# Two Mamba scans and a binarised convolution block on one core: another order of the kernel's head, and the convolutions' input in two float32r parts in place of three bf16 parts

## What is computed

```python
def _mamba(x, W_in, conv_w, conv_b, W_x, W_dt, b_dt, A_log, D_skip, W_out):
    xc, z = split(x @ W_in.T)                      # 256 features each
    xc = silu(causal_conv4(xc, conv_w) + conv_b)   # along 32 steps
    dbc = xc @ W_x.T                               # 8 for dt, 16 for B, 16 for C
    dt = softplus(dbc[..., :8] @ W_dt.T + b_dt)
    h = exp(dt * A) * h + (dt * xc) * B            # 16 states per feature, step by step
    y = (sum over states of h * C + xc * D_skip) * silu(z)
    return y @ W_out.T

def quantize_w1bit(w): return mean(abs(w)) * sign(w)
out = relu(batch_norm(x, gamma0, beta0))
out = conv3x3(out, quantize_w1bit(w0))
out = relu(batch_norm(out, gamma1, beta1))
out = conv3x3(out, quantize_w1bit(w1)) + x
```

## Time and profile before

| | |
|---|---|
| median of 3 runs | 888.1 us (886.25 to 889.18) |
| the profiled execution | 886.25 us, its span 884.5 us |
| mean granted TensorE clock | 0.959 of full speed |
| busy: PE, PEld, DVE, ACT, POOL | 777.8, 367.0, 764.4, 728.2, 707.7 us |

### The profile page before, as it was taken

One profiled execution on the slowest core, in us unless ns is written; L12 is line 12 of the kernel. 1 busy time (PEld: TensorE's weight loads), 2 busy tenths in 40 slices (PEclk: granted clock), 3 DMA queues, 4 the chain that ended last, 5 costly groups with the idle time before them and its releaser, 6 DMA issues.

```text
span 884.5 us, 13300 instructions
## 1 busy us (share of the span) xinstructions
PE 777.8 (88%) x4606; PEld 367.0 (41%) x4614; DVE 764.4 (86%) x504; ACT 728.2 (82%) x1305; POOL 707.7 (80%) x331
## 2 busy tenths in 40 slices
PE   5776989898999998989999989899999867689898
PEld 3433434343444443434544435354444334244343
DVE  2198999999999999999999999999999999871441
ACT  2798999999999999999999999999999995350310
POOL 0478899999999999999999999999999999300000
PEclk9888999999999999999999999999999987989999
DMA  6606152434242434443434344344444350000011
GB/s 191 253 36 241 49 182 107 177 136 185 106 176 114 167 124 154 159 156 134 151 138 146 144 130 184 126 164 128 161 122 168 113 200 1 1 1 1 0 48 48
DMA packets 39147, 110.99 MB, mean 125 GB/s; under 512 B 7244, under 2 KB 9384, under 8 KB 39080
## 3 DMA queue, kind: packets, MB, share of 16 engines
q1 hardware_dynamic: 36896, 109.81, 34.6%
q10 hardware_dynamic: 2184, 0.33, 0.2%
HBM read 106.97 MB, written 3.15 MB: 125 GB/s over the span
## 4 chain that ended last, share of the span: by engine, by line
DVE 39%; PE 21%; issue 19%; ACT 17%; POOL 2%; ACTq 0%; DMA 0%; POOLq 0%; DVEq 0%
DVE state L763 19%; DVE bank L763 15%; PE bank L1108 11%; ACT product L597 5%; ACT bank L573 4%; ACT state L584 4%; PE bank L959 3%; DVE state L773 2%; PE bank L952 2%; POOL state L511 2%; PE bank L1043 1%; PE bank L894 1%; ACT dt L627 1%; ACT L622 1%; PE bank L938 1%
## 5 line engine op out<-in xcount | busy, mean ns | idle before, releaser
L511 POOL TENSOR_TENSOR state<-state,c_wide 128x1024 f32<-128x1024 f32 x159 | 372.9, 2364 | 17.4 <-DVE state L763 17.3
L502 POOL TENSOR_TENSOR state<-u,b_wide 128x1024 f32<-128x1024 f32 x128 | 301.6, 2369 | 13.2 <-PE bank L959 7.4
L959 PE MATMUL bank<-state,ident 64*64 64x512 f32 x2048 | 260.8, 619 | 0.5 <-POOL state L511 0.5
L763 DVE TENSOR_TENSOR_SCAN state<-state,bank 128x1024 f32<-128x1024 f32 x95 | 214.8, 2271 | 0.7 <-ACT state L584 0.5
L597 ACT ACTIVATE product<-u_tok,b_tok 128x256 f32<-128x256 f32 x512 | 212.4, 497 | 2.3 <-PE bank L952 1.8
L952 PE MATMUL bank<-ident,product 128*128 128x128 f32 x1024 | 145.4, 288 | 77.1 <-ACT product L597 32.6
L952 PEld LDWEIGHTS bank<-ident,product 128*128 128x128 f32 x1024 | 117.4, 147 | 173.1 <-issue 92.7
L573 ACT ACTIVATE bank<-dt,a_neg 128x512 f32<-128x512 f32 x256 | 165.6, 677 | 26.3 <-DVE state L763 13.4
L584 ACT ACTIVATE state<-dt,a_neg 128x512 f32<-128x512 f32 x256 | 166.6, 711 | 0.2 <-PE bank L959 0.2
L763 DVE TENSOR_TENSOR_SCAN state<-bank,state 128x1024 f32<-128x1024 f32 x64 | 145.3, 2270 | 6.0 <-ACT bank L573 6.0
L763 DVE TENSOR_TENSOR_SCAN bank<-bank,state 128x1024 f32<-128x1024 f32 x64 | 146.2, 2284 | 1.1 <-ACT bank L573 0.3
(11 more groups left out here) (91 smaller groups left out, 529.1 us busy)
## 6 DMA issues: line engine op xcount, KB each, us to landing
c_wide<-bc_rows SPq DMA_DIRECT2D x128, 512.0 KB, 5.8
b_wide<-bc_rows SPq DMA_DIRECT2D x48, 512.0 KB, 7.6
b_wide<-bc_rows SPq DMA_DIRECT2D x32, 256.0 KB, 3.6
x_t<-in_x_dram SPq DMA_DIRECT2D x4, 512.0 KB, 4.9
out_dram<-x_t SPq DMA_DIRECT2D x8, 256.0 KB, 2.0
k_room<-in_L_conv_w_dram SPq DMA_DIRECT2D x2, 576.0 KB, 7.1
bc_rows<-dbc SPq DMA_DIRECT2D x16, 64.0 KB, 1.6
state<-in_L_conv_W_in_dram SPq DMA_DIRECT2D x2, 256.0 KB
```

The costliest lines, as they stand in the source:

```text
L502: pool.tensor_tensor(tile(n), u[:, :, :], over_halves(b_wide[:, PLAIN.index(s), :]), ALU.mult).then_inc(plain_input, 1)
L511: pool.tensor_tensor(tile(n), tile(n), over_halves(c_wide[:, n % NST, :]), ALU.mult).then_inc(output_pool, 1)
L763: dve.tensor_tensor_scan(flat(target), flat(decay), flat(source), 0.0, ALU.mult, ALU.add).then_inc(scanned, 1)
L959: return pe.matmul(y_sum[64 * h:64 * h + 64, b, :], weights[rows, :], source[rows, h, :], start=first, stop=last)
```

## The change

Loads: each kind has its own semaphore (taps: W_in and conv_w; small: W_x, the vectors, W_dt; A_log; W_out; three for x), and their order on the two queues is by use. The six loads of the convolution's kernels, gammas and betas go from ahead of item 0 to behind its spreads of B and C. Raw weights lie at the end of `state`, from slot 4 on, and only states 4 to 8 wait for their transposes. The order of groups is new, with two banks, five groups copied by ACT and the others by DVE; the skip diagonals and A's negation are on DVE. ACT makes the gates between the two halves of xc. In the last part there are two parts in float32r, in rows of 33 elements with a zero between rows, so that every tap takes full rows of 32; the sign matrices are cast to float32r by POOL in the last item.

```diff
-PARTS = 3
+PARTS = 2
+PADDED = W + 1
+PART = NB * H * PADDED + 2
-AT_SETUP = 7
-SETUP_LEAD = 2
+AT_EXACT = (11, 12)
...
+        wide = sb("wide", [128, len(PLAIN) + NST, CHUNK])
+        b_wide, c_wide = wide[:, 0:len(PLAIN), :], wide[:, len(PLAIN):, :]
+        room = wide[:, :, :].rearrange("p s n -> p (s n)")
+        k_exact = [room[:, n * TAPS * 128:(n + 1) * TAPS * 128].bitcast(F32R).rearrange("p (q e) -> p q e", e=128)
+                   for n in range(2)]
+        PARTS_AT = 2 * TAPS * 128
+        parts = [room[:, PARTS_AT + p * PART:PARTS_AT + (p + 1) * PART] for p in range(PARTS)]
...
         def wait_slot_free(eng, n):
             wait(eng, summed, n - SLOTS + 1)
+            if RAW_SLOT <= n < SLOTS:
+                eng.wait_ge(setup_mm, WEIGHT_GROUPS)
...
+        GROUPS = [x_group(0), *tap_groups(0), z_group(0), *small_groups(0), out_group(0),
+                  *tap_groups(1), z_group(1), *small_groups(1), out_group(1), *(x_group(g) for g in range(1, TOKENS // CHUNK))]
+        BY_ACT = (0, 2, 9, 11, 13)
+        GROUPS_FIRST, GROUPS_AT_TAPS, GROUPS_AT_DBC, GROUPS_AT_DT = range(0, 5), range(5, 7), range(7, 8), range(8, 14)
+        GROUPS_AT_B_TOK, GROUPS_AT_U_TOK = range(14, 16), range(16, NG)
-        SETUP_BANKS = 3
+        SETUP_BANKS = 2
...
         @block.sync
-            load_matrices(sp, 0)
-            load_x_tokens(sp, 1, 2)
-            load_matrices(sp, 1)
-            load_x_tokens(sp, 2, TOKENS // CHUNK)
+            load_w_in(sp, 0)
+            load_w_x(sp, 0)
+            load_x_tokens(sp, 1)
+            load_w_in(sp, 1)
+            load_conv_w(sp, 1)
+            load_x_tokens(sp, 2)
+            load_w_x(sp, 1)
+            load_vectors(sp, 1)
+            load_w_dt(sp, 1)
+            load_a_log(sp, 1)
+            for m in range(2):
+                load_w_out(sp, m)
...
         @block.scalar
-            load_x_tokens(act, 0, 1)
-            for m in range(2):
-                load_vectors(act, m)
+            load_conv_w(act, 0)
+            load_x_tokens(act, 0)
+            load_vectors(act, 0)
+            load_w_dt(act, 0)
+            load_a_log(act, 0)
+            act.preload_act_table_set("silu_and_others")
...
                         act.activation(xc[m][:, h, :], work[h], ACT.Silu, bias=conv_b[m][:, h:h + 1]).then_inc(xc_ready, 1)
+                        if k == 0 and h == 0:
+                            gates(0)
+                    if k == 0:
+                        act.preload_act_table_set("softplus")
...
         @block.gpsimd
+            def exact_weights(n):
+                pool.wait_ge(k_copied, 4)
+                wait(pool, plain_input, before(PLAIN, LAST))
+                pool.tensor_copy(k_exact[n], k_t[n][:, :, :]).then_inc(k_exact_ready, 1)
+            def pads():
+                wait(pool, plain_input, before(PLAIN, LAST))
+                for s in range(COVERED):
+                    wait_output(pool, LAST - NST + s)
+                for part in range(PARTS):
+                    pool.memset(parts[part][:, 0:PART:PADDED], 0.0).then_inc(pads_ready, 1)
-                    if k < 0 and NST * k + POOL_B.get(s, (0,))[0] == 0:
-                        pool.wait_ge(setup_mm, NG)
...
-                    dve.tensor_tensor(rest, full, inner(0, n), ALU.subtract).then_inc(act_rest, 1)
-                    dve.wait_ge(act_rest, g + 1)
-                    dve.tensor_copy(inner(1, n), rest).then_inc(act_mid, 1)
-                    dve.wait_ge(act_mid, g + 1)
-                    dve.tensor_tensor(inner(2, n), rest, inner(1, n), ALU.subtract).then_inc(act_lo, 1)
+                    dve.tensor_tensor(inner(1, n).bitcast(F32R), by_row(act_f[:, n % 2, :]), inner(0, n),
+                                      ALU.subtract).then_inc(act_lo, 1)
...
-                            mm = pe.matmul(bank[n].rearrange("p (r w) -> p r w", w=W)[:, dst[0], dst[1]], k_t[layer][:, q, :],
-                                           image(part, n // 2)[:, src[0], src[1]],
+                            mm = pe.matmul(by_row(bank[n])[:, dst, :], k_exact[layer][:, q, :],
+                                           shifted(part, q)[:, src, 0:W],
```

More of the change, by code:

```diff
@@ L10 @@
 BF16 = mybir.dt.bfloat16
+F32R = mybir.dt.float32r
 NB, C, H, W = 4, 128, 32, 32
@@ L325, in res_half, with load_x_tokens @@
             return res[n // 2][:, n % 2 * CHUNK:(n % 2 + 1) * CHUNK]
-        def load_x_tokens(eng, first, last):
+        X_PIECES = ((0, 1), (1, 2), (2, TOKENS // CHUNK))
+        def load_x_tokens(eng, piece):
             rows = x.rearrange("b c h w -> (b c h w)").rearrange("(a p d) -> p a d", p=128, d=D)
[L330 to L334, removed]
+            a, b = (4 * q for q in X_PIECES[piece])
+            eng.dma_start(x_tok[:, a:b, :], rows[:, a:b, :]).then_inc(load_x[piece], 16)
@@ L598, in products, with gates @@
                                    scale=b_tok[k % 2][:, blk, s:s + 1]).then_inc(product_ready, 1)
+            def gates(k):
+                wait(act, gated, HALVES * (k - 1))
+                for h in range(HALVES):
+                    wait(act, z_mm, 2 * k + h + 1)
+                    act.activation(gate[k % 2][:, h, :], z_place(k)[h], ACT.Silu).then_inc(gate_ready, 1)
             def prepare(k, s):
@@ L628, in prepare @@
                     act.preload_act_table_set("exp_and_others")
+                    if k == 0:
+                        for a in range(MAMBAS):
+                            a_log(a)
+                        for g in BY_ACT:
+                            if g in GROUPS_AT_DT:
+                                setup_copy(act, copy, g, setup_act)
                 if s == ACT_B_TOK:
@@ L880, in _, with target_half @@
         def _(pe):
+            def target_half(g):
+                return sum(GROUPS[q][:2] == GROUPS[g][:2] for q in range(g))
             def transposes(g):
                 what, which, sources, cols, _, _ = GROUPS[g]
-                last = g - SETUP_BANKS
-                if last >= 0:
-                    pe.wait_ge(setup_act if last % 2 == 0 else setup_dve, last // 2 + 1)
+                if g >= SETUP_BANKS:
+                    pe.wait_ge(*copied(g - SETUP_BANKS))
                 if what == "x":
-                    pe.wait_ge(load_x, 16 * X_LOADS[which])
-                else:
-                    pe.wait_ge(load_w[which], W_LOADS)
-                    pe.wait_ge(taps_ready, HALVES * (which + 1))
+                    pe.wait_ge(load_x[X_PIECE[which]], 16)
+                if what == "tap":
+                    pe.wait_ge(taps_ready, HALVES * which + target_half(g) + 1)
+                if what == "z":
+                    pe.wait_ge(load_taps[which], TAP_LOADS)
+                if what == "small":
+                    pe.wait_ge(load_small[which], SMALL_LOADS)
+                if what == "out":
+                    pe.wait_ge(load_out[which], OUT_LOADS)
                 for j, src in enumerate(sources):
@@ L928, in project @@
                 h, tap = part // KCONV, part % KCONV
+                if k == 1 and tap == 0:
+                    pe.wait_ge(*copied((8, 9)[h]))
                 if part == 0:
```

275 lines of the change are left out of this document (153 added, 122 removed).

## The result

| | before | the change |
|---|---|---|
| median | 888.38 us (4 runs, 886.25 to 889.18) | 858.92 us (4 runs, 857.70 to 859.51) |
| the profiled execution, its span | 886.25, 884.5 us | 859.51, 857.6 us |
| mean granted TensorE clock | 0.959 | 0.958 |

The ratio is 0.967, with a 95% interval of 0.965 to 0.969: 29.5 us less. Forecast were 850.7 us and a range of 846 to 862; the time lies inside the range, 8.2 us above the forecast and 2 us above 857, the end of the range that the forecast alone had.

What follows compares the result with a forecast made beforehand. DVE's gapless scans were taken as a fixed block, PE's matmuls as the last part's bound; -29.2 us (convolutions) and -8.2 (head) made -37.4 from 886.25, so 848.9, or 850.7 us for the median; range 846 to 862.

Steps and rivals of the forecast that it cites:

- The bound: DVE's gapless list from the first scan is a fixed block; only the head and the convolutions behind it can change.
- The price of a float32r column: Last part's matmuls: taken at the bf16 price, 0.432 ns a column, in one instruction; -29.2 us over 16 tiles.
- Rivals A: Last part: a float32r matmul takes two clocks a column, 7.78 us a tile, 912.9 us in all; chance 0.10.
- D: Last part: matmuls run as full float32, 1.70 ns a column, 15.3 us a tile, 1,034 us; chance 0.02.
- The term of 3.89 us: Last part: a tile's 9,024 columns at the bf16 price take 3.89 us in place of 5.72.
- the bound of 225 ns a matmul: Last part: the forecast's upper price, 225 ns in place of 216, giving -26.7 us in place of -29.2.
- Rival B: Last part: weight loads are not hidden, 6.2 to 7.27 us a tile, 888 to 905 us; chance 0.05.
- The head: Ahead of the scans: first scan at 36.2 us instead of 44.43, -8.2 us, bounds -4.4 and -10.7.
- the diagonals cost DVE under 1 us in time in which it waits for PE: 0: Head, DVE: making the skip diagonals there would not delay the first scan, 0 us.
- Rival C: Head's gain is lost through DVE's copies, a late load, ACT or new item 0 waits; 858.9 us; chance 0.07.
- the forecast's own signs: Whole kernel: statistics 3.9 us apart, matmuls about 216 ns, first scan near 36 us, no long DVE waits, casts in idle time.
- Nothing else late: POOL's casts, the zeros between rows and the later kernel loads are covered by idle time or early enough: 0 each.

Runs made afterwards that it cites:

- e1: The kernel before with only the change's float32r convolutions, its old head kept: 865.36 us, ratio 0.9727 to the kernel before.
- e8: The change with only the first 64 weight columns of each tap, half of the output channels left out: 858.79 us, one execution.
- e10: The change with seven rows (224 columns) in each convolution matmul, the rest of the sum left out: 112 ns from matmul to matmul, one execution.
- e9: The change with the three bf16 parts of the kernel before put back, so only the new head: 883.95 us, ratio 0.9935 to the kernel before.
- e3: The change with POOL's first multiplication by B held until all four skip diagonals are made: 857.18 us, one execution.
- e2: The change with the four skip diagonals back on ACT, behind b_tok: 856.10 us, ratio 0.9622 to the kernel before.
- e6: The change with diagonals on ACT, POOL's first multiplication by B behind A's negation, two x groups earlier: 854.99 us, ratio 0.9600 to the kernel before.
- e4: The change with the convolutions' input read as one contiguous run instead of rows at a distance of 33: 857.30 us, one execution.
- e7: e6 with eight transposes of the identity on PE while it waits for the first load: 855.21 us, ratio 0.9609 to the kernel before.

## Why the prediction was right, and where it was not

**The bound.** Right: the block from the first scan to the aggregation is 734.3 us before, 734.6 after and 734.4 in e1. DVE's list sets it, and the two ends were where the time went.

**The price of a float32r column.** Right in kind (one instruction a matmul, at a little over a quarter of float32's 870 ns), and short in size. Rivals A (0.86 ns a column) and D (1.7) are out: it is 4.19 us a tile. The term of 3.89 us assumed the bf16 price; 16 x 0.30 = 4.8 us of the sum were lost here, and the bound of 225 ns a matmul was too narrow beside 237. By e1 the last part is worth -24.2 in place of -29.2. A second error did no harm: I took the bf16 price from a division of a tile by its columns (0.432 ns), but rows cut to 31 elements cost the same as rows of 32 (216 ns at 496 and at 512 columns alike, 203 at 465 and 480). Full rows cost bf16 nothing more; at its own price the new tile would be 3.81 us (12 matmuls at 216 ns and 6 at 203), 0.08 under the forecast, and float32r takes 10% more than that.

**Rival B.** Out, by e8 and e10. What the prediction said of it, that loads hide under a longer matmul, holds within 1 ns at 512 columns and within 5 ns at 224. The load's own record grew from 98 to 189 ns in the steady part. The Trainium skill, page "TensorE: Matmul & The Clock Gate", section "Weight-path perf modes — Fast Weight Load (FWL) and DoubleRow", has fast loading off for FP32 weights; the trace agrees in the length of the load, and it costs no time here.

**The head.** -8.2 forecast, -5.4 measured in medians (e9). Up to dt the walk was good, even 1.2 us too slow: u starts at 26.04 us with slow taps and at 23.8 to 23.9 with quick ones, against 25.1 forecast. Behind u it was 5.0 us too short, 11.1 us against 16.1. The failed step is the one that said "the diagonals cost DVE under 1 us in time in which it waits for PE: 0", and the same holds for A's negation, which it did not price. The diagonals of layer 1 and A's negation took 6.7 us because POOL's multiplications by B, which the change starts 9.3 us earlier than before, hold them (e3). That was the collision to look for: an engine set free early, and what stands beside it. Its price is 2.9 us of first scan by e2 and, from u on, 2.8 by e3. Most of the rest is the copies of x: I took 0.75 us a group, the six took 6.2 (35.97 to 42.2), about one each. The timeline has PE at its lower level in that stretch; the windows of PE there (columns as in the earlier trace rows):

```profile
31.00:36.00 5.00, 2.36 (x11) 1.56 (x9) 5.00 (x5) 3.66 (x8) 4.53 (x2) 0.50 0.91 323
36.00:42.10 6.10, 6.10 (x27) 4.68 (x28) 4.46 (x7) 4.87 (x12) 0.00 (x0) 0.61 1.03 415
```

The trace of before had this level too (0.54 from 31 to 36 us, while it copied x), and the 1.04 us for eight transposes in the earlier trace rows that I used came from a quick stretch. In e3, with the same two banks, PE's clock is 1.00 from 35.1 to 38.1 us, and five copies take 0.71 us each:

```profile
34.66 3.57 DVE L455 COPY x_t<-bank 128x512 f32<-128x512 f32 x5 [0.16 <-PE bank L993]
```

So the pace of the copies goes with the level. That is read from the traces; no run changed the level in this stretch on purpose.

**Rival C** came true by a third, and its sign, a first scan after 40 us, was there at 42.12. DVE's copies did hold the first scan, but item 0 had no new wait above 0.8 us (its longest is 2.54 us at the kernels, before 3.0), and two thirds of the head's gain stayed. The missing 8.2 us against 850.7 are 5.0 of the convolutions, 2.8 of the head, and 0.4 that the two do not account for.

**What of the range was luck.** C's figure, 858.9 us, is the measured time, but it is made of -29.2 and 0, and the runs have -24.2 and -5.4: two errors happen to give the same sum. Of the forecast's own signs three had numbers that all were missed: 4.19 us a tile for 3.9, 237 ns for 216, the first scan at 42.1 us for 36. The range reached up to 862 because of C, while most of the miss is the price of the matmul, for which its bounds gave 2.5 us and which took 5.0. With all of C and the measured price the time would have been 863.9 us, outside. At the other end the range was also drawn loosely: by its own terms the forecast's range begins at 888.1 - 29.2 - 10.7 = 848.2 us, not at 847.

**The median.** The prediction put the profiled execution 1.85 us under the median and did not say why. It had quick taps, which by the first scans above is worth some 2 us. That is the likely reason, and not shown, since only the profiled execution has a trace.

**Nothing else late.** Right for the casts, the zeros and the kernels' loads, which took 13.0 us to land and were needed later.

A version that beats both kernels is e6, 854.99 us against 859.36 for the change on the same chip; e2 alone, with only the diagonals moved back, has 856.10.

## What to carry to other kernels

When an operation is moved to an engine that idles, look at who shares a path with it at that moment: DVE was idle and still the wrong place, because POOL was set free by the same change. Price a matmul in a new format by a short run of it before counting on it; here it could be argued from the trace that the price lies near bf16's, the last tenth could not. And compare heads of executions by their steps, not by one time: 2 us here come and go with one and the same code.

## What was not expected of the hardware

- Small DVE operations with their input in SBUF (128x32 and 128x64) stand still for whole POOL multiplications: 4.66 and 4.68 us for two, in the scalar and in the two-tensor form, against 0.41 with POOL held. DVE's copies from PSUM beside POOL's multiplications keep 0.69 us (e3). The Trainium skill, page "SBUF — State Buffer", section "Who interferes with whom", says so: a DVE instruction in a two-port mode, or one with two inputs in SBUF beside a GpSimd instruction that reads SBUF, contends with GpSimd, and one of them blocks for the whole instruction. The waits of both forms agree; which mode the scalar form ran in, no trace here shows. I had not brought it to bear on the diagonals.
- A float32r matmul of 512 columns comes every 237 ns beside bf16's 216, by the estimate above mostly a price per column; the stride of the rows is 3 ns of it and the weight load 1. Why a four-byte column costs 0.45 ns is not settled.
- In bf16, rows of 31 elements cost what rows of 32 do (216 ns at 496 and at 512 columns).
- The time of the first eight tap instructions differs by 2.1 us between executions of one list in the head (3.71 us in e4, 5.82 in e8), and eight more transposes ahead of them did not help (e7).
